# A fused FFN, attention, FFN kernel: the rope's sine product and sum issued on GpSimd in place of VectorE, with the planner's due times and horizon moved

## What is computed

```python
x = x + 0.5 * ffn(layernorm(x))      # r = sigmoid(xr W_r), k = relu(xk W_k)^2, out = r * (k W_v)
x = x + attn(layernorm(x))           # 16 heads of 16, rope on q and k, causal softmax
x = x + 0.5 * ffn(layernorm(x))
# rope: r0 = x0*cos - x1*sin ; r1 = x0*sin + x1*cos
```

## Time and profile before

| | |
|---|---|
| runs | 3033.27 us median (3032.0, 3033.27, 3041.44) |
| profiled execution | 3033.34 us, span 3031.6 us |
| PE | 2899.2 us busy, 96% |
| DVE | 2454.8 us, 81% |
| ACT | 2191.8 us, 72% |
| POOL | 1581.5 us, 52% |
| granted PE clock | 0.987 of full over the span |

### The profile page before, as it was taken

How to read it: one execution, slowest core, us unless ns; L and a number is a source line. 1 busy time by engine, 2 the same in 40 slices (tenths; PEclk the granted TensorE clock), 3 DMA queues, 4 the chain that set the end, 5 groups by cost and what they waited for, 6 DMA issues and landing times.

```text
span 3031.6 us, 56206 instructions
## 1 busy us (share of the span) xinstructions
PE 2899.2 (96%) x18245; PEld 1712.0 (56%) x18245; DVE 2454.8 (81%) x7302; ACT 2191.8 (72%) x4802; POOL 1581.5 (52%) x2190
## 2 busy tenths in 40 slices
PE   6797999999999999999999999999999999999997
PEld 4444555555656555555655655565565655565344
DVE  3885888888888888888888888888888888888862
ACT  4475777777777777777777777777777777777663
POOL 5454455555555555555655555555555555554322
PEclk9898999999999999999999999999999999999998
DMA  3424354344434434434433534443443543443411
GB/s 101 79 51 71 68 99 78 76 89 82 94 70 103 82 68 96 79 86 86 89 82 69 109 63 98 85 81 82 76 106 63 102 79 76 88 82 85 83 47 36
DMA packets 202585, 245.49 MB, mean 81 GB/s; under 512 B 68405, under 2 KB 104245, under 8 KB 202293
## 3 DMA queue, kind: packets, MB, share of 16 engines
q1 hardware_dynamic: 202293, 241.90, 39.1%
HBM read 53.48 MB, written 51.38 MB: 35 GB/s over the span
## 4 chain that ended last, share of the span: by engine, by line
PE 77%; DVE 13%; ACT 4%; issue 3%; POOL 1%; DMA 1%; SPq 1%; POOLq 0%; DVEq 0%; ACTq 0%
PE ps_y L977 17%; PE ps_s L946 14%; PE ps_m L956 13%; PE ps_d L1030 7%; PE ps_d L1033 7%; PE ps_d L1042 6%; PE ps_d L1036 6%; DVE ps_m L1183 4%; PE ps_d L1046 3%; DVE mx_sb L1186 3%; PE ps_d L1023 2%; ACT pt_sb L1072 2%; PE ps_d L984 2%; DVE ka_sb L1208 1%; DVE qb_sb L1241 1%
## 5 line engine op out<-in xcount | busy, mean ns | idle before, releaser
L1072 ACT ACTIVATE pt_sb<-ps_s 128x512 f32<-128x512 f32 (+1 forms) x2532 | 1221.4, 493 | 458.4 <-PE ps_s L946 431.2
L1183 DVE CUSTOM_DVE_ANT_0 ps_m<-ps_m,mask_sb 128x128 f32<-128x128 f32 (+3 forms) x2048 | 996.8, 497 | 332.7 <-PE ps_m L956 314.6
L956 PE MATMUL ps_m<-kr_sb,qr_sb 96*128 96x512 bf16 (+3 forms) x3072 | 1000.0, 329 | 52.9 <-DVE mx_sb L1183 17.6
L946 PE MATMUL ps_s<-qr_sb,kr_sb 99*128 99x512 bf16 (+1 forms) x3039 | 993.0, 329 | 30.9 <-ACT pt_sb L1072 20.7
L1186 DVE TENSOR_REDUCE mx_sb<-ps_m 128x1 f32<-128x512 f32 x1024 | 698.6, 682 | 96.4 <-PE ps_m L956 88.7
L1315 POOL TENSOR_SCALAR_AFFINE_SELECT pt_sb<-pt_sb 128x512 f32<-128x512 f32 x384 | 256.8, 669 | 531.7 <-ACT pt_sb L1072 529.0
L956 PEld LDWEIGHTS ps_m<-kr_sb,qr_sb 96*128 96x128 bf16 x3072 | 301.8, 98 | 372.9 <-DVE mx_sb L1183 51.6
L977 PE MATMUL ps_y<-pt_sb,v_sb 128*32 128x512 f32 (+2 forms) x5120 | 492.7, 493 | 3.8 <-POOL pt_sb L1315 3.5
L946 PEld LDWEIGHTS ps_s<-qr_sb,kr_sb 99*128 99x128 bf16 x3039 | 292.8, 96 | 330.8 <-issue 132.1
L1072 ACT ACTIVATE pn_sb<-ps_s 128x384 f32<-128x384 f32 x507 | 246.6, 492 | 216.2 <-PE ps_s L946 214.6
L1042 PE MATMUL ps_d<-axn_sb,wqk_sb 128*128 128x256 f32 x1024 | 312.7, 391 | 5.2 <-ACT axn_sb L1112 3.8
(11 more groups left out here) (113 smaller groups left out, 3891.5 us busy)
## 6 DMA issues: line engine op xcount, KB each, us to landing
kr_sb<-part_sb SPq DMA_DIRECT2D x378, 128.0 KB, 4.5
qr_sb<-part_sb SPq DMA_DIRECT2D x378, 128.0 KB, 4.8
y_way<-yt_sb SPq DMA_DIRECT2D x128, 256.0 KB, 2.3
sw_sb<-qb_sb SPq DMA_DIRECT2D x496, 64.0 KB, 2.0
x_sb<-x SPq DMA_DIRECT2D x64, 256.0 KB, 3.9
yn_sb<-y_way SPq DMA_DIRECT2D x64, 256.0 KB
den_sb<-r_way SPq DMA_DIRECT2D x64, 256.0 KB
out<-x_sb SPq DMA_DIRECT2D x64, 256.0 KB, 2.6
```

The costliest lines, as they stand in the source:

```text
L946: eng.matmul(score_bank(slot)[:, 0:width], kr_sb[0:KR + NP, n % RS, j, kb * P:(kb + 1) * P], qr_sb[0:KR + NP, n % RS, j, q0:q0 + width], s ...
L956: eng.matmul(ps_m[:, u % NM, 0:width], qr_sb[0:KR, n % RS, j, i * P:(i + 1) * P], kr_sb[0:KR, n % RS, j, piece * QC:piece * QC + width], s ...
L1072: eng.activation(buffer[:, j, column:column + width], score_bank(slot)[:, 0:width], ACT.Exp, scale=SCALE).then_inc(exped, 1)
L1183: eng.tensor_tensor_reduce(ps_m[:, u % NM, 0:width], ps_m[:, u % NM, 0:width], mask_sb[:, m0:m0 + width], 1.0, -3e38, ALU.add, ALU.max, be ...
```

## The change

`r_sin` and `r_add` are issued on POOL instead of DVE, with the same operands and waits. The hunks below leave out the two branches as they were in DVE's list. In the plan, their durations become 1350 and 1170 ns, they leave `SHARING`, and the predecessors carry no lag. Four planner numbers move: steps may start at most 45 slots (was 60) before they are due; the second FFN of a batch is due 20 slots earlier except for the last two batches; the first pair's rope of a later batch and its `r_QK` are due up to 20 slots earlier, the second pair's 10 to 16; and in batch 0 a step more than 25 slots late is placed even where it doesn't fit in the room left.

```diff
-             "r_cos": (1350, 1700), "r_sin": (610, 740), "r_add": (603, 740), "r_hi": (519, 680), "r_rest": (1170, 1500), "r_mid": (519, 680),
+             "r_cos": (1350, 1700), "r_sin": (1350, 1500), "r_add": (1170, 1330), "r_hi": (519, 680), "r_rest": (1170, 1500), "r_mid": (519, 680),
-    SHARING = ("f_k0", "f_k1", "f_r0", "f_r1", "r_sin", "r_add")
+    SHARING = ("f_k0", "f_k1", "f_r0", "f_r1")
-    EARLY_HEAD, EARLY = 16, 60
+    EARLY_HEAD, EARLY = 16, 45
+    LATE = 25
-            return at + BSLOTS + 70 + 24 * c
+            return at + BSLOTS + 50 + 24 * c
-                        t = (b - 1) * BSLOTS + (90 + 20 * c if pair else -10 + 18 * c)
+                        t = (b - 1) * BSLOTS + (80 + 18 * c if pair else -30 + 18 * c)
-                    s("DVE", "r_sin", i, 0.73, t, ("r_swap", i, 6))
-                    s("DVE", "r_add", i, 0.79, t, ("r_cos", i, 3), ("r_sin", i, 0))
+                    s("POOL", "r_sin", i, 1.2, t, ("r_cos", i, 0))
+                    s("POOL", "r_add", i, 1.2, t, ("r_sin", i, 0))
-            if early > slot or not self.ready(now - self.margin(e, slot), after) or e != "PE" and rank[0] == 2 and self.TAKES[name][0] + self.shut(name, now) > room:
+            if early > slot or not self.ready(now - self.margin(e, slot), after) or e != "PE" and rank[0] == 2 and not self.overdue(rank, slot) and self.TAKES[name][0] + self.shut(name, now) > room:
...
+    def overdue(self, rank, slot):
+        return slot < BSLOTS and rank[1] < slot - self.LATE
...
+                elif name == "r_sin":
+                    sin = sin_sb[:, halves(i % NCH)].rearrange("p (o n) -> p o n", o=1).broadcast_to([P, 2, CH])
+                    pool.wait_ge(swapped[i % NCH], 64 * (i // NCH + 1))
+                    eng.tensor_tensor(swapped_of(i), swapped_of(i), sin, ALU.mult).then_inc(r_sin, 1)
+                elif name == "r_add":
+                    pool.wait_ge(r_cos, i + 1)
+                    pool.wait_ge(r_sin, i + 1)
+                    eng.tensor_tensor(biased_of(i), biased_of(i), swapped_of(i), ALU.add).then_inc(r_add, 1)
```

More of the change, by code:

```diff
@@ L1233, in dense @@
                             eng.bn_aggr(amv_sb[:, t, :], ast_sb[:, t, :]).then_inc(a_mean, 1)
-                elif name == "r_sin":
-                    sin = sin_sb[:, halves(i % NCH)].rearrange("p (o n) -> p o n", o=1).broadcast_to([P, 2, CH])
-                    dve.wait_ge(swapped[i % NCH], 64 * (i // NCH + 1))
-                    eng.tensor_tensor(swapped_of(i), swapped_of(i), sin, ALU.mult).then_inc(r_sin, 1)
-                elif name == "r_add":
-                    dve.wait_ge(r_cos, i + 1)
-                    dve.wait_ge(r_sin, i + 1)
-                    eng.tensor_tensor(biased_of(i), biased_of(i), swapped_of(i), ALU.add).then_inc(r_add, 1)
                 elif name == "b_add":
```

## The result

| | before | after |
|---|---|---|
| runs, median | 3037.03 us (3032.0 to 3041.44, 4 runs) | 3058.35 us (3056.7 to 3066.24, 4 runs) |
| ratio | | 1.0077, 95% interval 1.0054 to 1.0100 |
| profiled execution | 3033.34 us | 3066.24 us |

What follows compares the result with a forecast made beforehand. PE was taken to bound the steady batches and DVE to set the pace in the head, with a hole at 251 us. The terms +5 - 8 - 10 - 3 - 2 = -18 gave 3015 us, 0.6% faster, range 3000 to 3030.

Steps and rivals of the forecast that it cites:

- The steady batches: Batches 2 to 13: DVE relief, emptier slots, due times and horizon together -2 us, bounds -10 and +10.
- Rival 3: DVE's own FFN products held up by a busier POOL; if all reached PE, +16 us, 3031 us; chance 0.06.
- The rule that I weighed: DVE instructions with both inputs in SBUF contend with POOL instructions reading SBUF; remaining pairs would meet more.
- Head: Up to batch 0's first full rows: POOL's longer chain makes them 5 us later, bounds 0 and +8.
- The stretch where DVE is the bound: First full rows to slot 32 (81 to 156 us): work leaving DVE gives -8 us, between -9 and 0.
- Hole: PE's wait at 251 us for batch 1's rows falls from 16.1 to 6 us: -10, between -18 and 0.
- the block: 17 dense products ahead of the wait at 251 us spread into other slots: -3 us, between -5 and 0.
- Rival 1: Selects come late behind POOL's products, 3 us a batch over 14 batches, 3057 us; chance 0.09.
- The signs I named: DVE near 2240 us, POOL near 1900, steady batch 179.3; wrong if above 180 or PE waits for selects.
- The end: The tail of the run keeps its order: 0 us.

Runs made afterwards that it cites:

- again: The changed kernel run once more, nothing edited: 3057.45 us, ratio to before 1.0074.
- guard: Changed kernel; POOL waits ahead of its next dense step until each group's finishing of the maxima (five small DVE steps) is through, from the fifth group: 3023.01 us.
- headdve: guard with r_sin and r_add of the first four chunks back on DVE: 3017.11 us, ratio to before 0.9933.
- besideset: Kernel before, with six POOL memsets of 128x200 added in the slot of the finishing of each batch's second group: 3033.37 us, ratio 0.9995.
- befguard: Kernel before, with only POOL's wait for each group's finishing of the maxima added, as in guard: 3036.75 us, ratio 0.9999.
- beside: Kernel before, with three POOL products of 128x200 added in the slot of the finishing of each batch's second group: 3044.94 us, ratio 1.0027.

## Why the prediction was wrong, point by point

The terms, each as a stretch between two rows of PE (changed kernel's profile, then `again`'s, less the profile before):

| stretch | forecast | measured |
|---|---|---|
| to the first full rows' maxima | +5 | +7.3, +5.5 |
| from there to the score of slot 32 | -8 | +3.7, -1.0 |
| slot 32 to slot 144 (hole and block) | -10 - 3 | -17.3, -15.7 |
| slot 144 to batch 2 | 0 | -0.2, -0.2 |
| batches 2 to 13 | -2, bounds -10 and +10 | **+30.7, +30.8** |
| batch 14 to the end | 0 | +8.4, +7.9 |

- **The step that failed is "The steady batches"**, put at -2 us with +10 as its worst; the runs showed +30.7, PE waiting for DVE's reductions behind a finishing that POOL's products hold up. The step weighed what DVE is relieved of, PE's waits for DVE (0.8 us in 200) and emptier slots, and set the bounds by "as much again appears". It never asked which DVE instruction stands ahead of the maxima and what POOL would run beside it. Five steps of 0.2 us each had no row in my argument, though the trace before had them once at 3.00 us together, with PE waiting 1.56 us behind. Without the collisions the term is about right: in `guard` the same batches take 3.2 us less than before. The cost of a collision isn't read from POOL's share of busy time: it is up to one product, 1.1 us, for each step, wherever the order lets them meet.
- **Rival 3** had the mechanism and the wrong instructions: it priced `f_k` and `f_r`, at +16 us in all and with a chance of 0.06. Over the whole run `f_k` did not grow (mean 0.711 us before, 0.701 after). `f_r` did, from 0.541 to 0.628 us, and one of them costs PE 0.8 us in each odd batch; `guard` keeps that wait. "That it reaches PE is against rows 3" was the error: those rows show the old order, in which, from batch 2 on, the two hardly met at the one place that matters.
- **The rule that I weighed**, the Trainium skill's SBUF — State Buffer, section Who interferes with whom, was the right one. I quoted it for steps with two inputs in SBUF. The same section of the Trainium skill also says that copies, casts and `tensor_scalar` can enter modes that take the shared ports, and that the blocked side waits for the whole instruction. The rows agree as to products of POOL: `TENSOR_SCALAR` 1.20 and `CAST` 1.18 us against 0.18. Whether a memset holds these two as well no run here shows.
- **Head**: mechanism right, within its bounds. `headdve` shows it.
- **The stretch where DVE is the bound**: wrong. From the first maxima to slot 32 it took 78.7 and 74.0 us, against 75.0. The term counted the 5.7 us that leave DVE's list and took its other steps to stay as long as they were. They didn't: in the changed kernel's profile the six `f_r` of this stretch grew from 3.7 to 6.1 us and the six `f_k` from 5.0 to 6.0 (in `again` `f_r` alone, to 5.1), beside a POOL busy for 43.4 us and not 34.3. DVE was relieved of 1.6 us (62.0 to 60.4). That is rival 3's mechanism, in the stretch where I had not looked for it. The two profiles of the change differ by the granted clock, 0.78 and 0.88 (before 0.86). That the longer `f_r` and `f_k` are what kept the time up is argued; nothing was run on it.
- **Hole**: right. 4.1 us of wait, forecast 6. With the block it gave 3 to 4 us more than forecast; the two were not measured apart.
- **Rival 1**, the slower one at a chance of 0.09, is out: PE's wait for selects is 2.2 us in the whole run, in two places.
- **The signs I named**: POOL 1853.8 us (forecast 1900): the pair took 333 us, near the 325 priced, but POOL's other steps 49 us less, among them cosine, select and `f_xadd` (1332 to 1308, 669 to 638 and 1410 to 1330 ns); DVE 2338.7 (2240), since rows of DVE overlap in the record, so that 214 us of rows taken out of the profile before take only 167 off the busy time, and since `f_r` and the finishing grew; a steady batch above 180 us was named as what would prove me wrong, and did.
- **The end**: +8 where 0 was forecast. 1.4 us is the wait in batch 14. Of the rest some is scatter: from batch 15's first score to the end, four kernels with the order of before (`before`, `besideset`, `befguard`, `beside`) took 202.6, 202.8, 207.1 and 207.2 us; here it is 209.6 and 207.5.

## What to carry to other kernels

When work is moved to GpSimd, list the short VectorE instructions with SBUF inputs that stand ahead of something TensorE waits for, and see what GpSimd will run beside each; each step of such a chain can be held once, to the end of one GpSimd instruction, whatever the busy shares (two or three of the five steps in the steady batches here). A wait of GpSimd for that chain is worth a try where GpSimd has room: here it cost GpSimd 1.1 us a time and made the kernel 34 us faster, and where there was nothing to guard it changed nothing. An experiment that adds work in a place has to show in its trace that the work ran in that place, before its time is read.

## What the runs showed that was not expected

- DVE steps with one input are held as well: `TENSOR_SCALAR` and `CAST` of 32 columns, 0.18 us alone, took 1.20 and 1.18 beside POOL's products of 128x512, and 0.54 and 0.47 beside those of 128x200.
- A wait of 2.38 us on PE is followed by 3.4 us at a granted clock of 0.5 in four of six cases, the same four in both profiles of the changed kernel, and those batches are 1.6 us longer. No wait of 1.41 us in the even batches was followed by a fall.
- The order's waits in the steady batches repeat to about a hundredth of a us from batch to batch and from run to run; what varies between runs of one kernel lies at the head and at the end.
